# Knn-graph blocks on one core: mixed products between the halves of the neighbour products, y high ahead of relu, high main products ahead of low

## What is computed

```
idx = top-8 nearest points of each point, from the squared distances of ctx_4096
for each of 2 layers, for i in range(4):          # 8 blocks in all
    p = leaky_relu(points, 0.01)
    g = p gathered at idx                          # 8 neighbours of each point
    points = (W[i] p + sum over the 8 of W[i] g) / 9 + points
```

## Time and profile before

| | us |
|---|---|
| three runs | 332.4, 334.34, 334.41 |
| their median | 334.34 |
| the profiled execution | 332.0 |
| its span, first to last instruction | 329.9 |
| around the span | 2.1 |
| TensorE busy | 316.8 (96%) |
| VectorE busy | 260.8 (79%) |
| ScalarE busy | 174.2 (53%) |
| GpSimd busy | 94.6 (29%) |

### The profile page before, as it was taken

How to read it: one execution, slowest core, us unless ns; L and a number is a source line. 1 busy time by engine, 2 the same in 40 slices (tenths; PEclk the granted TensorE clock), 3 DMA queues, 4 the chain that set the end, 5 groups by cost and what they waited for, 6 DMA issues and landing times.

```text
span 329.9 us, 5005 instructions
## 1 busy us (share of the span) xinstructions
PE 316.8 (96%) x1960; PEld 287.5 (87%) x1960; DVE 260.8 (79%) x333; ACT 174.2 (53%) x255; POOL 94.6 (29%) x85
## 2 busy tenths in 40 slices
PE   4999999999999898999899999999999999999995
PEld 4999999999998786887788888889888988889884
DVE  3994799899898938888868785987779868796773
ACT  4577197396384574546673645616555263644510
POOL 2011111111143323333633532416335053441400
DMA  7979949979920200000400000000000000000123
GB/s 225 351 222 252 243 143 235 234 255 224 247 52 17 50 0 0 2 0 0 63 3 0 3 1 2 0 0 2 0 2 0 0 2 0 2 0 2 43 86 128
DMA packets 17312, 25.50 MB, mean 77 GB/s; under 512 B 9476, under 2 KB 10756, under 8 KB 17288
## 3 DMA queue, kind: packets, MB, share of 16 engines
q1 hardware_dynamic: 15992, 20.46, 21.1%
q0 software_dynamic: 1296, 4.72, 7.9%
HBM read 20.98 MB, written 2.10 MB: 70 GB/s over the span
## 4 chain that ended last, share of the span: by engine, by line
PE 49%; DVE 4%; ACT 1%; issue 1%; DVEq 0%
PE wide L425 28%; PE wide L414 7%; PE wide L403 7%; PE wide L401 7%; DVE r_mixed L657 1%; DVE y_rest L717 1%; DVE y_lo L721 1%; DVE state L729 1%; ACT y_hi L565 1%; ACT relu L557 0%; DVEq L704 0%; ACT r_high L560 0%; DVEq L720 0%
## 5 line engine op out<-in xcount | busy, mean ns | idle before, releaser
L292 POOL TENSOR_TENSOR r_low<-relu,r_high 128x512 fp32r<-128x512 f32 x64 | 84.4, 1332 | 136.6 <-ACT r_high L560 136.6
L425 PE MATMUL wide<-adj,y_hi 128*128 128x512 f32 (+1 forms) x260 | 101.8, 393 | 0.8 <-DVE state L729 0.8
L425 PE MATMUL wide<-adj,y_lo 128*128 128x512 f32 (+1 forms) x260 | 101.9, 393 | 0.0
L717 DVE TENSOR_TENSOR y_rest<-wide,y_hi 128x1024 f32<-128x1024 f32 x32 | 39.2, 1224 | 43.0 <-ACT y_hi L565 43.0
L401 PE MATMUL wide<-w_high,r_high 128*128 128x256 f32 x256 | 62.1, 282 | 1.8 <-DVE y_rest L717 1.8
L557 ACT ACTIVATE relu<-state 128x512 f32<-128x512 f32 x64 | 40.2, 629 | 43.4 <-DVE state L729 30.8
L565 ACT CAST y_hi<-wide 128x1024 fp32r<-128x1024 f32 x32 | 32.2, 1007 | 56.3 <-PE wide L403 56.3
L403 PE MATMUL wide<-w_low,r_low 128*128 128x256 f32 x256 | 61.9, 281 | 0.0
L425 PEld LDWEIGHTS wide<-adj,y_hi 128*128 128x128 f32 x260 | 48.9, 188 | 11.2 <-DVE state L729 1.2
L425 PEld LDWEIGHTS wide<-adj,y_lo 128*128 128x128 f32 x260 | 49.0, 189 | 10.2
L401 PEld LDWEIGHTS wide<-w_high,r_high 128*128 128x128 f32 x256 | 48.3, 189 | 4.2 <-issue 1.8
(11 more groups left out here) (55 smaller groups left out, 276.9 us busy)
## 6 DMA issues: line engine op xcount, KB each, us to landing
raw<-in_ctx_dram SPq DMA_DIRECT2D x23, 512.0 KB, 5.3
g_low<-in_ctx_dram POOLq DMA_DIRECT2D x9, 512.0 KB, 7.7
state<-in_x_dram SPq DMA_DIRECT2D x4, 512.0 KB, 8.7
out_dram<-state SPq DMA_DIRECT2D x3, 512.0 KB, 2.8
w_raw<-in_fside_BxSxS_dram SPq DMA_DIRECT2D x1, 1024.0 KB, 12.0
rest_raw<-in_ctx_dram SPq DMA_DIRECT2D x4, 130.0 KB
raw<-in_ctx_dram SPq DMA_DIRECT2D x2, 256.0 KB, 3.0
turned<-nbr SPq DMA_TRANSPOSE x16, 4.2
```

Of the source, the lines that this page charges most:

```text
L292: nc.gpsimd.tensor_tensor(r_low[:, n % 3, h, :], relu[:, h, :], r_high[:, n % 3, h, :].bitcast(fp32), ALU.subtract).then_inc(r_low_ready, 1)
L425: mm = nc.tensor.matmul(bank[to][:, cols], part[:, s % 2, q, h * P:(h + 1) * P], adj[:, b, q, cols], start=(q == 0 and part is y_hi), stop ...
L717: nc.vector.tensor_tensor(y_rest[:, :, :], wide[MAIN][:, :].rearrange("p (q o) -> p q o", q=NB), y_hi[:, s % 2, :, :].bitcast(fp32), ALU.s ...
```

## The change

On TensorE the step is now: main products of s, first half of `out_step(s-1)`, mixed products of s, second half of `out_step(s-1)`. The 16 main products run as 8 high ones, which wait only for r_high, and then 8 low ones, which wait for r_low; the start mark is set once per bank. ScalarE does `y_high(s)` ahead of `relu_parts(s+1)`. VectorE does y_rest, `update(s-1, 0)`, y_lo, `update(s-1, 1)`, `relu_mixed(s+1)`. The last step's products go to banks 6, 7 and 0, and wait only for the updates of step 29. Step 0 keeps its order. No instruction is added or removed.

```diff
-        LAST_OUT = ((0, ALL, 4), (1, slice(0, N // 2), 5), (1, slice(N // 2, N), 0))
+        LAST_OUT = ((0, ALL, 6), (1, slice(0, N // 2), 7), (1, slice(N // 2, N), 0))
...
-            def y_step(s, w):
+            def y_main(s, w):
...
-                pe.wait_ge(r_low_ready, CH * s + CH)
+                pe.wait_ge(r_high_ready, CH * s + CH)
                 if s > 0:
                     pe.wait_ge(y_rest_ready, s)
-                for q in range(NB):
-                    dst = wide[MAIN][:, q * C:(q + 1) * C]
-                    for h in range(CH):
-                        nc.tensor.matmul(dst, r_high[:, s % 3, h, q * P:(q + 1) * P], w_high[:, w, h, :],
-                                         start=(h == 0), stop=False)
-                        mm = nc.tensor.matmul(dst, r_low[:, s % 3, h, q * P:(q + 1) * P], w_low[:, w, h, :],
-                                              start=False, stop=(h == CH - 1))
+                for part, weights in ((r_high, w_high), (r_low, w_low)):
+                    if part is r_low:
+                        pe.wait_ge(r_low_ready, CH * s + CH)
+                    for q in range(NB):
+                        for h in range(CH):
+
+                            mm = nc.tensor.matmul(wide[MAIN][:, q * C:(q + 1) * C],
+                                                  part[:, s % 3, h, q * P:(q + 1) * P], weights[:, w, h, :],
+                                                  start=(part is r_high and q % 2 == 0 and h == 0),
+                                                  stop=(part is r_low and q % 2 == 1 and h == CH - 1))
                 mm.then_inc(main_done, 1)
+
+            def y_mixed(s, w):
...
-                    out_step(s - 1, STEPS[s - 1][1], out_pieces(s - 1))
+                    first_half, second_half = out_pieces(s - 1)
+                    out_step(s - 1, STEPS[s - 1][1], [first_half])
+                    y_mixed(s, l % BLOCKS)
+                    out_step(s - 1, STEPS[s - 1][1], [second_half])
...
-            pe.wait_ge(state_ready, CH * LAST_STEP)
-            out_step(LAST_STEP, STEPS[LAST_STEP][1], LAST_OUT)
+            pe.wait_ge(state_ready, CH * (LAST_STEP - 1))
+            out_step(LAST_STEP, STEPS[LAST_STEP][1], out_pieces(LAST_STEP))
...
             for s in range(B * LAYERS):
+                y_high(s)
                 if s + 1 >= B - 1 and s + 1 <= LAST_STEP:
                     relu_parts(s + 1)
-                y_high(s)
...
             for s in range(B * LAYERS):
-                split_y(s)
+                y_remainder(s)
+                if s > 0:
+                    update(s - 1, 0, ALL, 2 * out_at(s - 1), 0)
+                y_low(s)
...
                 if s > 0:
-                    update(s - 1, 0, ALL, 2 * out_at(s - 1), 0)
+                    update(s - 1, 1, ALL, 2 * out_at(s - 1) + 1, 1)
                 if B - 1 <= s + 1 <= LAST_STEP:
                     relu_mixed(s + 1)
-                if s > 0:
-                    update(s - 1, 1, ALL, 2 * out_at(s - 1) + 1, 1)
```

More of the change, by code:

```diff
@@ L147, in out_at @@
             return FIRST_WIDE if s < ENTER or s % 2 == 0 else SECOND_WIDE
+        assert out_at(LAST_STEP) == SECOND_WIDE
         def by_dma(b, k):
@@ L418, in out_step @@
             def out_step(s, b, pieces):
-                for n, (h, cols, to) in enumerate(pieces):
+                for n, (h, cols, to) in pieces:
                     for q in range(NB):
@@ L430, in out_pieces @@
             def out_pieces(s):
-                return LAST_OUT if s == LAST_STEP else tuple((h, ALL, 2 * out_at(s) + h) for h in range(CH))
+                return enumerate(LAST_OUT if s == LAST_STEP else ((h, ALL, 2 * out_at(s) + h) for h in range(CH)))
             for b in range(B):
@@ L463, in _ @@
             for s, (l, b) in enumerate(STEPS):
-                y_step(s, l % BLOCKS)
+                y_main(s, l % BLOCKS)
+                if s == 0:
+                    y_mixed(s, l % BLOCKS)
                 if s == 0:
@@ L710, in add_selves, with y_remainder @@
                 nc.vector.tensor_tensor(nbr_diag, nbr_diag, eyes[:, :, :], ALU.add).then_inc(self_added, 1)
-            def split_y(s):
+            def y_remainder(s):
                 dve.wait_ge(y_hi_ready, s + 1)
@@ L718, in split_y, with y_low @@
                                         y_hi[:, s % 2, :, :].bitcast(fp32), ALU.subtract).then_inc(y_rest_ready, 1)
+            def y_low(s):
                 dve.wait_ge(mixed_done, s + 1)
```

## The result

Four runs of the changed kernel took 323.19 to 323.68 us, median 323.34, beside a median of 333.62 for the kernel before. The ratio is 0.9697, with a 95% interval of 0.9665 to 0.9728: 3.0% faster. Taken from the 334.34 that the forecast started from, that is 324.2 (323.1 to 325.2). The profiled execution took 323.19, with a span of 321.4, where the forecast said 323.9 and 321.8 for it.

A forecast was written before the change was run, and what follows sets the result against it. A ScalarE-VectorE loop held TensorE above its 6.58 us step floor; gains of 7.2 (6.4 in 28 steps, 0.8 at step 3) and 0.9 at the end sum to 8.1, taking 334.34 to 326.2 us, range 323.5 to 331.

The forecast's parts named there:

- the floor of a step: TensorE's main, mixed and output products in a step that waits for nothing: 6.58 us, 184.2 over 28 steps.
- The loop: ScalarE and VectorE, steps 3 to 8: y_hi, y_rest, y_lo, r_mixed, second update, relu, next y_hi set a 7.15 us period.
- the three-step return: A batch returns after three steps, closing the ScalarE-VectorE loop: always up to step 8, every third step later, losing some 0.25 us.
- the 6.4 us: Time lost in waits in stage two, steps 3 to 31: 190.66 us measured against a floor of 184.2.
- E: End of the main products of step s on TensorE, from which the prediction counts all times; y_hi was to start there.
- 0.15 late in every step: TensorE's next main products if all wait for r_low; high products first saves this, some 4 us over 28 steps.
- the junction at steps 2 and 3: Where step 3's main products start: 124.2 instead of 125.16, less a 0.1 wait for r_low, gaining 0.8 us.
- The end: Last output products, in banks 6 and 7, begin at E + 4.69 without the wait for the update: 0.9 us less.
- GpSimd as the loop: Slower rival: r_low at 1.95 us each makes steps 7.15, total 342; slower than before from 1.1 more in the chain; chance 4%.
- three more boundaries: Little-change rival: TensorE pays 0.1 at each of three added group boundaries a step, 8.7 us, giving 334.9; chance 5%.
- The half gain: Rival: a 0.1 to 0.2 wait stays each step, at low products or before y_lo, 4.2 us back, 330; chance 12%.
- the change without effect: Rival: VectorE's order makes the second update late for relu, so the wait stays, 332 to 334; chance 3%.

The follow-up runs named there:

- the halves alone: Kernel before, with output products cut in two around the mixed products and VectorE's new order, relu still ahead of y_hi: 328.25 us, ratio 0.9859.
- the run with relu first: Changed kernel with ScalarE's old order, relu ahead of y_hi: 327.46 us, ratio 0.9835, span 325.2.
- the longer r_low: Changed kernel with GpSimd doing the subtraction of the first half twice, once into a spare buffer: 350.27 us, ratio 1.0514.

## Why the prediction was right, and where it was not

**The bound.** The prediction called 6.58 the floor of a step. Measured are 6.56 and 6.58 in turn, 27 times without a wait, and 6.79 in step 3 with its wait for r_low. The 28 periods took 184.18 against 184.2: the wait in step 3 and the floor, 0.01 too high, cancel.

**The loop.** That y_hi, y_rest, y_lo, r_mixed, the second update and relu made the 7.15 was argued from rows. The runs bear it out in part: with y_hi ahead of relu the wait for r_mixed was gone in all steps; with the halves alone, relu still behind the update, the steps without the search fell to 6.57, though every third of them has the three-step return. No run took VectorE's order alone.

For the steps from 9 on the prediction's reading is only half of it. It put their losses (0.23 to 0.30, seven times) down to the three-step return alone. The rows of the kernel before at step 12, the first of the seven:

```profile
187.38 2.54 POOL L292 TENSOR_TENSOR r_low<-relu,r_high 128x512 fp32r<-128x512 f32 x2 [0.80 <-ACT r_high L560]
...
189.21 1.79 DVE L657 SCALAR_TENSOR_TENSOR r_mixed<-r_low,r_high 128x1024 fp32r<-128x1024 f32 x1
...
191.06 1.20 PE L414 MATMUL wide<-w_mixed,r_mixed 128*128 128x256 f32 x8
```

The return makes r_mixed late, and r_low of the next step, which runs until 189.92, then makes it long. At 1.22 it would have ended at 190.43, before the main products did (189.03 + 1.90 = 190.93), and the mixed products would not have waited. All seven such steps, and step 8 with its period of 7.73, have an r_mixed of 1.79 to 1.81. By this count some 2.4 of the 6.4 us (seven losses, 1.8, and 0.6 in step 8) also hang on VectorE and GpSimd meeting; no run took that away by itself.

**y_hi ahead of relu.** "Worth 7.15 down to whatever comes next" was right, but the next thing was mis-sized. The prediction set E equal to y_hi's start and so had r_low whole at E + 4.85; measured, 5.03. Its sign that y_hi starts within 0.1 of E failed for the same reason: it is 0.20 in every late step. It had a slack of 0.8 before the low products; the changed kernel has 0.6. The forecast stood because that slack took up the 0.2. By itself this edit costs 2.2%, 340.39 us beside 333.13.

**High products first.** "0.15 late in every step", "some 4 us over 28 steps", is the term that failed: measured are 0.50 a step and 14.0 us (the spans, 337.7 and 321.4, differ by more, of which 1.1 is stage one and 1.1 the junction at step 3). On top of the 0.16 come 0.18 from the signal, 0.06 to the first matmul and 0.1 for a group after a stall. The sum of the forecast didn't rest on it, as with the edit in place there is no wait either way.

**Mixed between the halves.** All times of VectorE's list held within 0.2: at 173.45, 174.59, 175.21, 177.09 and 177.70, with E at 172.20, against E + 1.05, 2.3, 3.0, 4.95 and 5.6 (read 1.25, 2.39, 3.01, 4.89, 5.50). Cover held everywhere. What the prediction saw only in part is how the edits lean on one another. It did say that high products first counts given y_hi first; the runs show besides that ScalarE's order alone is slower, that it needs the high products first, and that VectorE's order with the mixed products left in place gives all back. The smallest set tried that gives most (2.1 of 3.0% by the ratios, 6.1 of 8.5 us by the spans) is ScalarE's order with the high products first.

**The junction and the end.** Step 3 began at 124.11 (124.2), waited 0.2 for r_low (0.1), step 31 at 308.29 (308.6), the last output products at 314.87 (315.2). The end alone gave 0.9, as worked out.

**GpSimd and VectorE.** r_mixed was to take 1.22 in each step. Its line, all 32 of them (minimum, median, maximum in ns):

```profile
L670 DVE SCALAR_TENSOR_TENSOR r_mixed<-r_low,r_high x32: 1211/1215/1226, 103.4 to 309.1; 128x1024 fp32r<-128x1024 f32 x32
```

Before, the longest was 1.81 us. So the rule of the Trainium skill, "SBUF — State Buffer", "Who interferes with whom", that a VectorE instruction with two SBUF inputs and a GpSimd instruction that reads SBUF contend, was seen at work on both sides: r_mixed is not lengthened where r_low is over before it starts, and takes 2.19 where relu goes first. The prediction weighed it for the order with y_hi first only; for the other order it would have pointed to the steps of 7.0, four by 0.43, 1.7 of the 3.8 us of span that the run with relu first lost.

**The rivals.** GpSimd as the loop was placed rightly: the longer r_low made 7.36. Its break-even of 1.1 us more in the chain was too high: with 0.6 of slack, 0.1 for the stall, and 0.3 a step to lose, it is about 0.8, an estimate from these runs. TensorE paid nothing for three more boundaries. The half gain and the change without effect didn't come. The chance of 0.89 for over 1% is a slip: the 0.76 and the 0.12 that it is made of give 0.88 at most.

**The size.** The forecast of 326.2 was 2 us above the 324.2 of the ratio; the median as measured, 323.34, lies just under the lower end of its range, 323.5. The span was right within 0.4, so the miss is the level: the prediction carried the 2.3 us between the profiled execution of before (332.0) and the median (334.34) over to the changed kernel. In later runs the kernel before took 331.69 to 334.73, and the changed one stayed within 0.5 us. Some of it may lie in stage one: its end moved by 1.8 us among the profiled executions. Why the changed kernel's four runs are all at the low end isn't settled.

## What to carry to other kernels

Where several engines pass a step around, work out for each buffer when it is ready and when it is wanted, counted from one point of the busiest engine, and add the signal (0.2 us here) and the slower start after a stall (0.1) to each link. An edit that cuts one loop is worth the distance to the next one and can be negative by itself: here y_hi ahead of relu cost 2.2% until the products that don't need r_low went first. When an engine's list is reordered, look at which instructions of two other engines now fall together, not only at who waits for whom.

## What was not expected of the hardware

A first group behind a wait takes 0.1 us more than one that follows on: 16 main products 2.0 and not 1.9 us. From the end of the main products, read as the start of the group behind them, to the start of y_hi on ScalarE pass 0.2 us (172.20 to 172.40). VectorE's r_mixed and GpSimd's r_low took turns: in the run with the halves alone the first r_low ran from 134.95 to 136.25; r_mixed, begun at 135.13, ended at 137.32, which is 1.07 behind it; the second r_low, begun at 136.62, ended at 138.46, 1.14 behind r_mixed. The instruction that is held up reads longer (2.19 for 1.22 after an overlap of 1.12, 1.84 for 1.30 after one of 0.70), with no idle time before it, so no list of waits shows it. The Trainium skill, "SBUF — State Buffer", "Who interferes with whom", states that the two contend and that one of them blocks, and the rows agree.
